# Inverse joins on four quarters of TensorE, with a new order of the steady slot

## The reference

```python
q, k, v = silu(dwconv(x @ Wq)), silu(dwconv(x @ Wk)), silu(dwconv(x @ Wv))   # 16 heads of 128
alpha, beta = sigmoid(x @ Wa + ba), sigmoid(x @ Wb + bb)
def step(S, inp):                      # 256 tokens, one after the other
    qt, kt, vt, at, bt = inp
    err = einsum('bhvk,bhk->bhv', S, kt) - vt
    S = at * S - bt * err * kt
    return S, einsum('bhvk,bhk->bhv', S, qt)
o = layernorm(o) * ln_w + ln_b
return (o * sigmoid(x @ Wg)) @ Wo
```

## Time and profile before

| | us |
|---|---|
| median of 3 runs | 3179.25 |
| the profiled execution | 3174.32 |
| its span | 3172.5 |
| PE busy | 2712.6 (86%) |
| DVE busy | 2251.3 (71%) |
| ACT busy | 2126.5 (67%) |
| POOL busy | 2001.5 (63%) |

### The profile page before, as it was taken

How to read it: one execution, slowest core, us unless ns; L and a number is a source line. 1 busy time by engine, 2 the same in 40 slices (tenths; PEclk the granted TensorE clock), 3 DMA queues, 4 the chain that set the end, 5 groups by cost and what they waited for, 6 DMA issues and landing times.

```text
span 3172.5 us, 65475 instructions
## 1 busy us (share of the span) xinstructions
PE 2712.6 (86%) x21872; PEld 2201.8 (69%) x21872; DVE 2251.3 (71%) x5574; ACT 2126.5 (67%) x4995; POOL 2001.5 (63%) x2171
## 2 busy tenths in 40 slices
PE   6889889646679999999999999999999999976761
PEld 4555555425568888888888888888888888765651
DVE  5777777575546767767767677677677676688877
ACT  4767776324458778777777777777787787754531
POOL 3544554333766878677786776868768777676432
PEclk9999999667889999999999999999999999988976
DMA  2000000014577676776767767677676767633311
GB/s 98 0 0 0 0 0 0 3 56 126 119 205 193 163 201 156 190 195 160 203 149 192 195 162 197 159 189 191 167 182 173 188 178 176 160 87 88 86 29 53
DMA packets 750313, 402.07 MB, mean 127 GB/s; under 512 B 406867, under 2 KB 686163, under 8 KB 749910
## 3 DMA queue, kind: packets, MB, share of 16 engines
q1 hardware_dynamic: 750038, 398.59, 48.6%
HBM read 263.80 MB, written 134.62 MB: 126 GB/s over the span
## 4 chain that ended last, share of the span: by engine, by line
PE 52%; ACT 6%; DVE 5%; POOL 4%; issue 3%; SPq 0%; DMA 0%; DVEq 0%; POOLq 0%; ACTq 0%
PE bank L2041 22%; PE bank L2092 8%; PE bank L2208 7%; PE bank L2072 4%; PE bank L2156 4%; ACT acc L1116 2%; POOL oT L896 2%; ACT shifted L1114 2%; PE bank L2080 2%; PE bank L2198 1%; PE bank L2126 1%; PE bank L2135 1%; PE bank L2114 1%; ACT oT L1191 1%; ACT TT L1171 1%
## 5 line engine op out<-in xcount | busy, mean ns | idle before, releaser
L863 POOL TENSOR_TENSOR acc<-acc,shifted 128x510 f32<-128x510 f32 x384 | 557.4, 1452 | 455.8 <-DVE acc L1637 455.8
L1637 DVE SCALAR_TENSOR_TENSOR acc<-bank,conv_w,acc 128x254 f32<-128x254 f32 (+1 forms) x1536 | 630.6, 472 | 271.3 <-ACT acc L1116 270.9
L2041 PE MATMUL bank<-x_k,w_kq 128*128 128x256 f32 x2048 | 509.5, 399 | 25.1 <-DMA x_k<-xT_scratch 25.1
L1114 ACT ACTIVATE shifted<-bank,conv_w 128x255 f32<-128x255 f32 x768 | 368.0, 479 | 178.6 <-issue 113.6
L2041 PEld LDWEIGHTS bank<-x_k,w_kq 128*128 128x128 f32 x2048 | 388.5, 197 | 90.2 <-issue 15.2
L1116 ACT ACTIVATE acc<-bank,conv_b,conv_w 128x256 f32<-128x256 f32 x768 | 439.9, 573 | 0.0
L776 POOL TENSOR_TENSOR prob<-prob,rinv 128x512 f32<-128x512 f32 x192 | 202.0, 1055 | 265.9 <-DVE rinv L1433 265.7
L880 POOL TENSOR_TENSOR inv<-inv,outer 128x30 f32<-128x30 f32 (+14 forms) x480 | 287.6, 599 | 37.6
L1660 DVE TENSOR_TENSOR LM<-bank,dec 128x512 f32<-128x512 f32 x256 | 167.7, 687 | 155.7 <-PE bank L2072 146.6
L2208 PE MATMUL bank<-w_o,oT 128*128 128x256 f32 x1024 | 247.3, 386 | 24.5 <-POOL oT L896 23.7
L877 POOL TENSOR_TENSOR outer<-inv 128x30 f32<-128x30 f32 (+14 forms) x480 | 242.7, 506 | 35.6 <-DMA inv<-D_scratch 8.0
(11 more groups left out here) (243 smaller groups left out, 5905.5 us busy)
## 6 DMA issues: line engine op xcount, KB each, us to landing
abc<-decay_scratch SPq DMA_DIRECT2D x64, 512.0 KB, 5.3
MTm<-M_scratch SPq DMA_DIRECT2D x128, 256.0 KB, 3.4
kqm<-q_scratch SPq DMA_DIRECT2D x64, 512.0 KB, 4.6
knm<-k_scratch SPq DMA_DIRECT2D x64, 258.0 KB, 3.2
x_k<-xT_scratch SPq DMA_DIRECT2D x64, 256.0 KB, 2.9
q_scratch<-kq SPq DMA_DIRECT2D x128, 128.0 KB, 2.7
q_scratch<-kq SPq DMA_DIRECT2D x64, 256.0 KB, 3.4
D_scratch<-LM SPq DMA_DIRECT2D x256, 64.0 KB, 2.4
```

The lines of the kernel that those rows point to most:

```text
L863: pool.tensor_tensor(dst, dst, shifted[:, u % 2, :, 1:], ALU.add).then_inc(Z["sumk" if u < 4 else "sumv"], 1)
L1114: act.activation(shifted[:, u % 2, i % 2, 1:], pj[:, 0:SEQ - 1], ACT.Copy, scale=conv_w[:, kind, bass.ds(head, 1), TAPS - 2:TAPS - 1].rear ...
L1637: dve.scalar_tensor_tensor(out=acc[:, kind, i, t:], in0=pj[:, 0:SEQ - t], scalar=wcol, in1=acc[:, kind, i, t:], op0=ALU.mult, op1=ALU.add) ...
L2041: mm = pe.matmul(dst[:, i * SEQ:(i + 1) * SEQ], w[:, k, head * DK:(head + 1) * DK], x[:, k, :], start=(k == 0), stop=(k == CT - 1))
```

## The change

1. **Quarters.** For chunk 1 the output of `join("y")` goes to the other row half, and `join("x")` brings it back. With the loop order heads, chunks, halves, four matmuls in a row lie on the four quarters. The loads of `Cc` on SP place chunk 1's blocks accordingly. `joined` now makes one copy per chunk and half, four of 64x128 where there were two of 64x256.
2. **PE order.** `state` goes ahead of `second_out`, `proj_v(1)` directly follows `proj_v(0)`, `keys` goes ahead of `first_out`, and `outT(0)` ahead of `queries_on_state`.
3. **ACT order.** The copy of the state goes ahead of `gate(0)`, `keys` between the two `affine`, `from_state` ahead of `silu(2)`, and `first_out` between the two `values`.
4. **DVE order.** `second_rhs` goes ahead of `products(p, 3)`.
5. **POOL shares.** Piece 0 gets nothing. In kinds 1 and 2 piece 1 and piece 2 get two elimination steps each instead of one, and piece 3 gets more.

```diff
-SHARE = (2, 4, 2, 1, 1, 4, 2, 1, 1, 4, 2, 0)
+SHARE = (2, 5, 0, 2, 2, 5, 0, 2, 2, 4, 0, 0)
@@ SP, load_y
-                    solved(Cc, inv_dram, x, c, (1, 3), slice(0, BLK), Z["ld_y"])
+                    solved(Cc, inv_dram, x, c, ((1, 3), (3, 1)) if c else ((1, 1), (3, 3)), slice(0, BLK), Z["ld_y"])
@@ ACT, joined
-                    for m in range(2):
-                        src = bank[JOIN_BANKS[m]][rows_of(m), c0 * HG * BLK:c1 * HG * BLK]
-                        act.copy(dst[rows_of(m)].rearrange("p c h t -> p (c h) t"), src.rearrange("p (n t) -> p n t", t=BLK)).then_inc(Z[step + "e"], 1)
+                    for c in range(TPS):
+                        if (hn, h)[c] is not None:
+                            for m in range(2):
+                                to = m ^ c if step == "y" else m
+                                frm = m if step == "y" else m ^ c
+                                src = bank[JOIN_BANKS[frm]][rows_of(to), c * HG * BLK:(c + 1) * HG * BLK]
+                                ins = act.copy(dst[rows_of(to), c, :, cols], src.rearrange("p (h t) -> p h t", t=BLK))
+                                ins.then_inc(Z[step + "e"], 1)
@@ PE, join
-                    for c in range(TPS):
-                        if (hn, h)[c] is not None:
-                            for i in range(HG):
+                    for i in range(HG):
+                        for c in range(TPS):
+                            if (hn, h)[c] is not None:
                                 for m in range(2):
+                                    frm, to = (m, m ^ c) if step == "y" else (m ^ c, m)
-                                    mm = pe.matmul(bank[JOIN_BANKS[m]][rows_of(m), at0:at0 + BLK], lhsT[rows_of(m), c, i, :], rhs[rows_of(m), c, i, :],
+                                    mm = pe.matmul(bank[JOIN_BANKS[frm]][rows_of(to), at0:at0 + BLK], lhsT[rows_of(frm), c, i, :], rhs[rows_of(frm), c, i, :],
@@ DVE, steady slot
-                    conv(5), decays(p), products(p, 0), products(p, 1), products(p, 2), products(p, 3)
+                    conv(5), decays(p), products(p, 0), products(p, 1), products(p, 2)
                     if h is not None:
                         second_rhs()
+                    products(p, 3)
```

More of the change, by code:

```diff
@@ L495, in solved @@
                     need(sp, Z["st_w"], 32 * (x // BATCH) + 32)
-                    for i in places:
+                    for to, i in places:
                         at0 = i * BLK + (x % BATCH) * PROBS + c * HG
-                        sp.dma_start(dst[quarter(i), c, :, cols],
+                        sp.dma_start(dst[quarter(to), c, :, cols],
                                      src[x // BATCH][at0:at0 + HG, :].rearrange("b (r e) -> r b e", e=BLK)).then_inc(signal, 16)
@@ L1166, in joined @@
                     act.wait_ge(Z[step + "p"], past(s - LAG_V + 1))
-                    c0, c1 = 0 if hn is not None else 1, TPS if h is not None else 1
-                    dst = Yb[:, c0:c1, :, 0:BLK] if step == "y" else TT[:, c0:c1, :, BLK:]
-                    for m in range(2):
-                        src = bank[JOIN_BANKS[m]][rows_of(m), c0 * HG * BLK:c1 * HG * BLK]
-                        act.copy(dst[rows_of(m)].rearrange("p c h t -> p (c h) t"), src.rearrange("p (n t) -> p n t", t=BLK)).then_inc(Z[step + "e"], 1)
+                    dst, cols = (Yb, slice(0, BLK)) if step == "y" else (TT, slice(BLK, HB))
+                    for c in range(TPS):
[6 more added lines that the diff above has]
+                                ins.then_inc(Z[step + "e"], 1)
                 def first_out():
@@ L1212, in slot @@
                     if h is not None:
-                        gate(0), state()
+                        state(), gate(0)
                     tap(4), tap(5)
@@ L1218, in slot @@
                     if n is not None:
-                        affine(0), affine(1)
-                    keys(p), silu(2)
+                        affine(0)
+                    keys(p)
+                    if n is not None:
+                        affine(1)
                     if h is not None:
-                        first_out(), from_state()
-                    values(0), values(1)
+                        from_state()
+                    silu(2), values(0)
+                    if h is not None:
+                        first_out()
+                    values(1)
                 else:
@@ L2109, in solve_upper @@
                     pe.wait_ge(Z["ld_t"], past(32 * halves(s, LAG_H)))
-                    pe.wait_ge(Z["xe"], past(2 * (s - LAG_V)))
+                    pe.wait_ge(Z["xe"], past(2 * halves(s - 1, LAG_V)))
                     def tile(c, i, m, cols):
@@ L2171, in second_out @@
                     if joining(s):
-                        pe.wait_ge(Z["xe"], past(2 * (s - LAG_V) + 2))
+                        pe.wait_ge(Z["xe"], past(2 * halves(s, LAG_V)))
                     else:
@@ L2233, in slot @@
                     join("x"), proj_k(2), proj_k(3)
+                    if middle:
+                        state()
                     if rear:
@@ L2237, in slot @@
                         proj_g(0)
-                    proj_v(0)
+                    proj_v(0), proj_v(1)
                     if middle:
-                        state()
-                    proj_v(1)
+                        proj_g(1), keys_on_state()
+                    keys(p)
                     if middle:
-                        proj_g(1), keys_on_state(), first_out()
-                    keys(p)
+                        first_out()
+                    if rear:
+                        outT(0)
                     if middle:
@@ L2247, in slot @@
                     if rear:
-                        outT(0), outT(1)
+                        outT(1)
                     products(p, 0), products(p, 1), products(p, 2)
```

8 lines of the change are left out of this document (4 added, 4 removed).

## The result

The changed kernel takes 3160.94 us (median of 5 runs, 3158.72 to 3162.22), the kernel before 3178.84 us (5 runs beside it). The ratio is 0.9941, 95% interval 0.9928 to 0.9955: faster by 0.6%, where I had forecast 3198 us and slower. The profiled execution took 3159.97 us, its span is 3158.2 us. Most of the difference lies in the steady slots (s = 10 to 63): 1798.1 us against 1808.4. In the drain (s = 64 to 72) it is 296.9 against 305.3 us. The start of s = 10 is 1.1 us later (952.05 against 950.99), and what follows the start of s = 73 takes 111.0 us against 107.8.

What follows compares the result with a forecast made beforehand. PE looked like the bound, but a loop through POOL set kinds 0 and 1. +1.6 us per turn gave +21.6, filling and drain -3, so +19: 3193 profiled, 3198 us median; range 3145 to 3225.

Steps and rivals of the forecast that it cites:

- the sum per turn: Change over four steady slots, one of each kind: +1.15 + 1.0 + 0.1 - 0.65 = +1.6 us, times 13.5 turns +21.6.
- Chain to `second_out`: From the joins through ACT's taps and copies: y join 0.47 us faster, four copies 1.10 us, second_out 0.13 us earlier.
- rival C: No change: the chain to second_out shrinks by 0.5 instead of 0.13 us, the turn's sum is about 0, 3179 us; chance 0.14.
- POOL from `powers` to `project_out(0)`: Kind 1: a second elimination step and DVE's holds on POOL start project_out(0) at +29.1 against +27.92, costing +1.15 us.
- Kind 2: Slot with the same POOL stretch as kind 1 but smaller rectangles: +1.0 us.
- Kind 0: Slot with the same four elimination steps before and after; the scan may catch one operation more: -0.1 to +0.4, taken as +0.1.
- Kind 3: Slot without that elimination: gated(0) ends at +26.8, project_out(0) starts at +26.95 instead of +27.61, -0.65 us.
- Rival A: Faster: POOL does not decide, PE does, reaching project_out(0) at +26.85 in kinds 1 to 3; 3136 us, chance 0.27.
- the loop through piece 2: From join x through second_out, powers, POOL's elimination and gated(0) to PE's tail; said to set the slot in kinds 0 and 1.
- the single-chunk row: Profile row of a join with 16 records in 0.60 us; basis for 32 records on four quarters taking 0.60 instead of 1.07.
- rival B: Slower still: the joins get no faster because quarters sharing a row half load one after the other; 3223 us, chance 0.11.
- own range: Span given to the 3198 us forecast itself: 3188 to 3210 us, chance 0.48.

Runs made afterwards that it cites:

- e12: Kernel after with the x join alone in its old loop order (chunks outside, heads inside); 3160.43 us.
- e11: Kernel after with DVE's scan over one head instead of four from slot 16 on; 3098.14 us.
- e7: Kernel before with no elimination in piece 2 on POOL; 3152.2 us.
- e5: Kernel before with the new order of PE, ACT and DVE only, joins and shares as before; 3165.39 us.
- e1: Kernel after with the old POOL shares of the elimination; 3137.8 us.
- e3: Kernel after with no elimination in piece 2 on POOL; 3091.61 us.
- e8: Kernel before with the new joins and copies and no elimination in piece 2, old order; 3127.36 us.
- e2: Kernel before with the new joins and four narrow copies alone, old order and shares; 3158.71 us.
- e4: Kernel after with the old joins and two wide copies, so new order and shares only; 3194.32 us.
- e6: Kernel after with the old order of the steady slot, new joins and shares; 3172.7 us.
- e10: Kernel after with gated(0) ahead of add_shifted(4) on POOL; 3160.35 us.
- e9: Kernel after with no elimination in piece 2 and none in kind 3 (shares 0,6,0,3,0,6,0,3,0,5,0,0); 3113.19 us.

## Why the forecast was wrong

The mechanism was right and its size was off: the term that failed is the sum per turn, +1.6 us forecast and -1.0 measured. With 13.5 turns this is -13.5 instead of +21.6 us, a miss of 35 of the 37 us between forecast and result. (Two slots at a lower clock take 3 us of that back. The medians account for 4 more: they stand 1.0 us above the profiled execution, where I had 4.9. The rest outside the steady slots came to -4 us where I had -3.) By kind:

| kind | forecast | measured | miss |
|---|---|---|---|
| 0 | +0.1 | -0.57 | 0.67 |
| 1 | +1.15 | +0.49 | 0.66 |
| 2 | +1.0 | +0.22 | 0.78 |
| 3 | -0.65 | -1.15 | 0.50 |

- **Chain to `second_out`: 0.2 us in every kind.** I wrote that behind `tap(1)` ACT "works without a gap" and that "the x join's saving does nothing here". It has a gap of 0.2 us ahead of `tap(2)`, which waits for `proj_k(2)` behind both joins. It went away, and this chain shrank by 0.32 instead of 0.13 us. That the x join's saving removed this gap is read from the rows; e12, which was to show it, did not lengthen the join enough. In kinds 1 and 2 the joins are worth 0.31 to 0.33 us in all four pairs of kernels that differ in them alone, in either order. This was rival C's condition, in part.
- **POOL from `powers` to `project_out(0)`: 0.46 us in kind 1.** Behind `powers` I had 2.4 and 1.35 us for the steps, 2.2 + 1.26 for the hold and `add_shifted(4)`, 1.26 for `gated(0)`. From start to start the rows have 2.30, 1.30, 3.23 and 1.22. The scan's hold is 2.0 (3.26 - 1.26) and not 2.2, the hold of `normalise` 0.87 (1.52 - 0.65) and not 1.1, and a row starts 0.03 to 0.05 us before the end of an addition ahead of it. These are errors of 0.04 to 0.23 in one direction, four times, 0.42 together.
- **Kind 2.** I let its smaller rectangles (198 and 184 elements instead of 234 and 238) count for 0.29 us against kind 1 (+28.81 and +29.1). They make it 0.39 us shorter.
- **Kind 0.** I took +0.23 for a further operation held by the scan. None was; 0.25 us went the other way.
- **Kind 3.** `gated(0)` ended at +26.3 where I had +26.8, and was still the last, by some 0.3 us (e11). PE would have been there at +26.19. Rival A's +26.85 for PE in this kind does not follow from its own 1.0 us: 27.61 - 1.0 is +26.6.

A reading that was wrong without moving the sum: I wrote that in kind 1 before, the loop through piece 2 sets the slot. The earlier trace rows say otherwise: `gated(0)` stands idle for 1.41 us until ACT's `affine(0)`, which waits for `outT` on PE. With an empty piece 2 (e7) it starts at +25.49, just as before. With the new order (e5) it starts at +23.94 without a wait, and kinds 1 and 2 get 0.59 us shorter. So the order, of which I costed all moves but `state` at nothing, opened POOL's row there, and the second elimination step filled it again. No run moves `outT(0)` alone. The forecast counted its row from `powers` on, so the wait was not in it.

What held. The joins take 0.62 us, as forecast from the single-chunk row. The copies take 1.11 us (1.10 forecast). `state` moves into the wait. PE waits 2.34, 1.89 and 1.60 us for `gated(0)` in kinds 0, 1 and 2. That POOL's second step costs, e1 shows. `second_out` started at +11.75 (forecast +11.9) and the scan at +23.4 (forecast +23.8 to 24.2), both a little early. That piece 2 stands on the path, e3, e7 and e8 show, and that the scan holds POOL, e11. With this rival A falls, and rival B with the joins' 0.62 us. The drain gained 8.4 us where I had 3 for filling and drain together, and 3.2 us were lost again behind it, which I did not follow either. In pairs that differ in the joins alone it is 3.3 to 7.3 us (e5 to e1, before to e2, e4 to after, e7 to e8), and 2.6 to 4.3 in pairs that differ in the shares (e5 to e4, e2 to e6, e1 to after). That POOL's pieces reach into the drain I had not counted. The path of this gain I did not follow.

What I should have seen is the balance: a forecast of +19 us was the difference of terms of up to 1.5 us per slot with 54 repeats, and 0.65 us per slot turned its sign. In kind 1, 0.42 of that is the error of four durations that I added up. The own range of 22 us was too narrow for that.

## What to carry to other kernels

Find the loop that closes last by its own stretches (here `project_out(0)` to the next join is the same 8.37 us in nearly every version, and the others carry the change), and ask for each which wait ends last in it. Where PE waits for POOL, empty POOL's row before making PE faster: joins and order were worth 61 us with an empty piece 2 and 41 with the shares of before (some 55 without the long slots of kind 0), and the change's own shares left 18 of them. When a sum of small terms is multiplied by 54, give its sign only the certainty of the worst term.

## What the runs showed of the hardware

**The clock after a long wait.** In kernels in which PE waits 2.34 us for `gated(0)` in kind 0, some of these slots take up to 1.7 us more: 2 of 13 after, 8 of 13 in e1, 11 of 13 in e5, 10 of 13 in e4, 1 of 13 in e12. (In e11 only s = 12 has that wait, and it is such a slot.) Windows in such a slot of the kernel after (s = 12): the whole slot, PE's wait, and 2.3 us that begin 2.0 us behind it; granted clock in the third column from the end.

```profile
1017.26:1053.00 35.74, 32.80 (x269) 28.16 (x268) 23.68 (x60) 26.52 (x59) 22.59 (x25) 0.95 0.75 187
1043.26:1045.95 2.69, 0.36 (x2) 0.01 (x1) 2.41 (x7) 0.00 (x0) 2.69 (x5) 1.00 1.08 327
1047.95:1050.26 2.31, 2.31 (x8) 1.74 (x6) 0.00 (x0) 0.28 (x1) 2.31 (x4) 0.50 1.06 358
```

The clock is full during the wait and falls to 0.50 (1.2 GHz) while PE is busy behind it; PE's busy time in the slot grows from 31.1 to 32.8 us. None of the kernels in which PE's waits in the steady slots stay at 1.8 us or below shows such a slot (before, e2, e3, e6 to e8, e10). But in e9, s = 62 takes 34.38 us instead of 33.06, at a clock of 0.95, behind waits of 0.35 and 1.23 us that end 2.4 us apart. And the waits of 1.91 and 1.60 us in kinds 1 and 2 (after, e4, e12) have none behind them. So the length of a single wait does not decide alone, and why it strikes 2 slots in one kernel and 11 in another with the same wait, nothing here tells. It costs e1 some 14 us, e4 some 17 and e5 some 19 (8, 10 and 11 times 1.7), so these show less than their orders and shares are worth, and it adds 3 us to the kernel after.

**Small matmuls on four quarters.** 32 records take 0.62 us, and the next matmul starts 0.55 us after the join's first. That is 17 ns per record on average, and one chunk's 16 records still take 0.60 to 0.65 us. The rule that I weighed in the prediction, from the Trainium skill, "TensorE: Matmul & The Clock Gate", section "Wait — 56ns, not 53.3ns?", that starts come no closer than about 25 ns, does not hold here, for records on different quarters: by it 32 starts would take 0.8 us. In e12, with chunks outside and heads inside, the same 32 take 0.89 us, where the kernel before needed 1.07 with two quarters that lie on the diagonal; I did not expect that and did not test why.
